# The last layer's weights padded to the full array, and the state's turn spread over VectorE and GpSimd, in a two-stage feed-forward of a four-stage layer kernel

## What is computed

```python
def ffn(x, ...):                      # x: [8, 1024, 256], normalized
    gf = global_net(x.mean(axis=1, keepdims=True), ...)       # one number per batch
    out = x
    for _ in range(3):
        h = gelu(out @ w1 + b1)       # 256 -> 256
        h = gelu(h @ w2 + b2)         # 256 -> 128
        h = gelu(h @ w3 + b3)         # 128 -> 64
        tf = sigmoid(h @ w4 + b4)     # 64 -> 1: one number per token
        c = 0.1 + adaptive_range * (0.7 * gf + 0.3 * tf - 0.5) * 2.0
        o_r, o_i, p_r, p_i = split(out, 4)
        out = out + c * concat([p_r, -p_i, -o_r, o_i])
    return out
```

## Time and profile before

| | |
|---|---|
| time of three runs | 3188.64, 3192.45, 3194.84 us; median 3192.45 |
| profiled execution | 3188.64 us; span from first to last instruction 3186.8 us |
| granted TensorE clock, mean of the span | 0.961 |
| busy in the span | TensorE 2836.8 us (89%), ScalarE 2018.3 (63%), VectorE 1842.2 (58%), GpSimd 1304.6 (41%) |
| the two ffn stages | about 950 to 1336 us and 2798 to 3187 us of the span |

### The profile page before, as it was taken

The page is one execution under the profiler, slowest core; times in us unless marked ns, Lnnn a source line. Parts: engine busy times, 40 slices in busy tenths (PEclk is TensorE's granted clock), DMA queues, the critical chain, the costliest instruction groups (busy, mean ns, idle before and its releaser), DMA issues. The chain is left out here.

```text
span 3186.8 us, 38521 instructions
## 1 busy us (share of the span) xinstructions
PE 2836.8 (89%) x12161; PEld 1226.6 (38%) x12161; DVE 1842.2 (58%) x2419; ACT 2018.3 (63%) x2642; POOL 1304.6 (41%) x795
## 2 busy tenths in 40 slices
PE   1799999999988999655999999999999999969998
PEld 0355555555553444331323232323333332234443
DVE  7899999999974453454354444444534442044444
ACT  4554555455434555424979797888878888935554
POOL 7699898889872220051313132222213230021210
PEclk8899999999998999867999999999999999989999
DMA  2000011001003220205463553545462717231112
GB/s 79 0 30 27 23 39 33 26 20 39 20 24 110 67 66 29 88 14 109 51 133 54 103 85 78 92 85 93 72 115 47 126 27 146 27 113 42 64 53 66
DMA packets 164017, 200.46 MB, mean 63 GB/s; under 512 B 16504, under 2 KB 118272, under 8 KB 163840
## 3 DMA queue, kind: packets, MB, share of 16 engines
q1 hardware_dynamic: 163840, 198.25, 28.2%
HBM read 139.49 MB, written 58.72 MB: 62 GB/s over the span
## 5 line engine op out<-in xcount | busy, mean ns | idle before, releaser
L1819 ACT ACTIVATE b_pr<-b_ps 128x1024 f32<-128x1024 f32 x1024 | 1003.0, 1025 | 256.0 <-PE b_ps L1916 251.6
L1916 PE MATMUL b_ps<-b_st 128*128 128x512 bf16 x2048 | 591.8, 386 | 71.1 <-DMA b_st<-b_scratch 33.9
L1898 PE MATMUL b_acc<-b_pr,b_vaug 128*32 128x512 f32 x4096 | 548.6, 608 | 0.4 <-ACT b_pr L1819 0.4
L1916 PEld LDWEIGHTS b_ps<-b_st 128*128 128x128 bf16 x2048 | 150.5, 98 | 649.2 <-ACT b_pr L1819 380.3
L1217 PE MATMUL f_po<-f_s,f_w 128*128 128x512 f32 x768 | 352.0, 600 | 10.1 <-DVE f_xr L1002 6.3
L990 DVE TENSOR_TENSOR f_turned<-f_cs,f_s 128x1024 f32<-128x1024 f32 x96 | 119.4, 1244 | 364.7 <-ACT f_cs L1119 359.7
L604 PE MATMUL a_pv<-a_xnT,a_wv 128*128 128x512 f32 x512 | 249.9, 612 | 48.2 <-DVE a_mem L389 31.4
L596 PE MATMUL a_pu<-a_xnT,a_wk 128*128 128x512 f32 x512 | 237.4, 607 | 36.2 <-DVE a_frac L350 30.3
L1083 ACT ACTIVATE f_h<-f_po,f_b 128x512 f32<-128x512 f32 x192 | 131.9, 687 | 215.8 <-PE f_po L1217 215.8
L1535 POOL TENSOR_TENSOR b_SQ<-b_A 128x1024 f32<-128x1024 f32 x32 | 64.7, 2022 | 466.9 <-DVE b_A L1632 466.9
L643 PE MATMUL a_py<-a_wo,a_out 128*128 128x256 f32 x960 | 228.3, 381 | 0.0
(11 more groups left out here) (247 smaller groups left out, 4659.2 us busy)
## 6 DMA issues: line engine op xcount, KB each, us to landing
b_st<-b_scratch SPq DMA_DIRECT2D x512, 128.0 KB, 6.9
b_scratch<-b_parts SPq DMA_DIRECT2D x32, 768.0 KB, 8.2
f_xl<-x SPq DMA_DIRECT2D x16, 1024.0 KB, 5.5
f_xr<-x SPq DMA_DIRECT2D x16, 1024.0 KB, 6.8
a_xl<-in_L_attn_a_x_dram SPq DMA_DIRECT2D x16, 512.0 KB, 4.3
x<-a_xr SPq DMA_DIRECT2D x32, 256.0 KB, 2.2
x<-f_xr SPq DMA_DIRECT2D x8, 1024.0 KB, 4.5
b_xl<-x SPq DMA_DIRECT2D x8, 1024.0 KB, 7.7
```

What stands on the lines that cost most here:

```text
L1819: nc.scalar.activation(pr[:, 4 * (blk % 2) + j, :], ps[:, j % 2, :], ACT.Exp, scale=SC).then_inc(S["probs_done"], 1)
L1898: x = nc.tensor.matmul(acc[32 * j:32 * j + 32, h * 512:(h + 1) * 512], vaug[:, kt, c:c + 32], pr[:, 4 * (kt % 2) + j, h * 512:(h + 1) * 51 ...
L1916: x = nc.tensor.matmul(ps[:, j % 2, h * 512:(h + 1) * 512], st[:, g % 2, 1, j, kt * P:(kt + 1) * P], st[:, g % 2, 0, j, h * 512:(h + 1) * ...
```

## The change

- w4r becomes two tiles of 128 rows, each with w4 on one half of the partitions and zeros on the other; GpSimd clears it first. L4's matmuls then use all 128 rows of the array and of h3.
- The coupling moves from ScalarE (L1119) to VectorE, as a tensor_scalar ahead of the turn.
- The turn no longer makes both products in one instruction. VectorE makes the product for row 0 right into the next state and adds to it; GpSimd makes the product for row 1 into the next state, and VectorE subtracts it from the state. GpSimd waits for the coupling, VectorE's subtract waits for GpSimd (b_done).
- GpSimd's turns stand in its queue in the order of the steps, between the normalizations; the last pair, in which GpSimd had nothing to do, has turns now too.
- `turned` and `couple` are gone.

```diff
-        w4r = s.sb("w4r", [P, P])
+        w4r = s.sb("w4r", [P, 2, P])
...
-        turned = s.sb("turned", [P, 2, KD, HT])
...
+                nc.gpsimd.memset(w4r[:], 0.0).then_inc(setup_p, 1)
...
+                def turn(x, k, j):                                          # GpSimd
+                    for h in range(NH):
+                        c = slice(h * HT, (h + 1) * HT)
+                        pool.wait_ge(cs_done[x], 6 * j + 2 * k + h + 1)
+                        nc.gpsimd.tensor_tensor(S[k + 1][:, x, 1, c], cs[:, x, c], S[k][:, x, 0, c],
+                                                ALU.mult).then_inc(b_done[x], 1)
+
                 def pair(j, first=False, last=False):
                     for step, x, k in ffn_steps(first, last):
+                        if step in ("L34", "L4"):
+                            turn(x, k, j - 1 if (x, k) == (1, 2) else j)
                         if step == "LN":
                             norm(x, j + 1)
...
+                pair(PAIRS - 1, last=True)
+                turn(1, 2, PAIRS - 1)
...
-                def turn(x, k, j):
+                def turn(x, k, j, end=False):                               # VectorE
...
-                        dve.wait_ge(cs_done[x], n + 1)
+                        dve.wait_ge(act_done, PRO + ACT_TILES * (j + (1 if (x, k) == (1, 2) else 0)) + (h + 2 if end else l34_at(x, k, 1 + h) + 1))
+                        dve.wait_ge(k2_done, j + 1)
...
-                        nc.vector.tensor_tensor(turned[:, h], cs[:, x, c].unsqueeze(1).broadcast_to([P, KD, HT]), src[:, x, :, c],
-                                                ALU.mult).then_inc(product_done[x], 1)
-                        dve.wait_ge(product_done[x], n + 1)
-                        nc.vector.tensor_tensor(dst[:, x, 0, c], src[:, x, 0, c], turned[:, h, 1, :], ALU.add)
-                        nc.vector.tensor_tensor(dst[:, x, 1, c], src[:, x, 1, c], turned[:, h, 0, :], ALU.subtract).then_inc(state_done[x], 1)
+                        nc.vector.tensor_scalar(cs[:, x, c], th[:, x, c], k1, k2[:, x:x + 1], ALU.mult, ALU.add).then_inc(cs_done[x], 1)
+                        dve.wait_ge(cs_done[x], n + 1)
+                        nc.vector.tensor_tensor(dst[:, x, 0, c], cs[:, x, c], src[:, x, 1, c], ALU.mult).then_inc(a_done[x], 1)
+                        dve.wait_ge(a_done[x], n + 1)
+                        nc.vector.tensor_tensor(dst[:, x, 0, c], dst[:, x, 0, c], src[:, x, 0, c], ALU.add)
+                        dve.wait_ge(b_done[x], n + 1)
+                        nc.vector.tensor_tensor(dst[:, x, 1, c], src[:, x, 1, c], dst[:, x, 1, c], ALU.subtract).then_inc(state_done[x], 1)
...
-                nc.vector.tensor_scalar(w4r[:], ones[:], w4c[:], None, ALU.mult).then_inc(setup_v, 1)
+                for h in range(2):
+                    r = slice(h * M3, (h + 1) * M3)
+                    nc.vector.tensor_scalar(w4r[r, h, :], ones[r, :], w4c[r, :], None, ALU.mult).then_inc(setup_v, 1)
...
-                    nc.scalar.activation(th[:, x, c], p, ACT.Tanh, scale=0.5, bias=hb4).then_inc(act_done, 1)
-                    act.wait_ge(k2_done, j + 1)
...
-                    nc.scalar.activation(cs[:, x, c], th[:, x, c], ACT.Identity, scale=k1, bias=k2[:, x:x + 1]).then_inc(cs_done[x], 1)
...
                 def l4(x, h, bank):
-                    r = slice(h * M3, (h + 1) * M3)
-                    nc.tensor.matmul(po[:, bank, :], w4r[r, :], h3[r, x, :], start=True, stop=True).then_inc(tile_ready, 1)
+                    nc.tensor.matmul(po[:, bank, :], w4r[:, h, :], h3[:, x, :], start=True, stop=True).then_inc(tile_ready, 1)
```

More of the change, by code:

```diff
@@ L825, in phase_f @@
         cs_done = [s.sem(f"cs_done{x}") for x in range(2)]
-        product_done = [s.sem(f"product_done{x}") for x in range(2)]
+        a_done = [s.sem(f"a_done{x}") for x in range(2)]
+        b_done = [s.sem(f"b_done{x}") for x in range(2)]
         state_done = [s.sem(f"state_done{x}") for x in range(2)]
@@ L1036, in _ @@
                 dve.wait_ge(w_loaded, N_W)
-                dve.wait_ge(setup_p, 4)
+                dve.wait_ge(setup_p, 5)
                 dve.wait_ge(setup_v, 2)
@@ L1044, in _ @@
                 nc.vector.tensor_scalar(hgb3, hgb3, 0.5, None, ALU.mult).then_inc(setup_v, 1)
-                nc.vector.tensor_scalar(w4r[:], ones[:], w4c[:], None, ALU.mult).then_inc(setup_v, 1)
+                for h in range(2):
+                    r = slice(h * M3, (h + 1) * M3)
+                    nc.vector.tensor_scalar(w4r[r, h, :], ones[r, :], w4c[r, :], None, ALU.mult).then_inc(setup_v, 1)
                 nc.vector.tensor_scalar(gw3r[0:M3, :], ones[0:M3, :], gw3c[0:M3, :], None, ALU.mult).then_inc(setup_v, 1)
-                dve.wait_ge(setup_v, 9)
+                dve.wait_ge(setup_v, 10)
                 pair(0, first=True)
@@ L1051, in _ @@
                 pair(PAIRS - 1, last=True)
-                turn(1, 2, PAIRS - 1)
+                turn(1, 2, PAIRS - 1, end=True)
                 for x in range(2):
@@ L1094, in pair @@
                                 p = take(j, at + h + (step == "L34"))
-                                couple(x, h, 6 * jj + 2 * k + h, jj, p, PRO + ACT_TILES * j + l34_at(x, k, 1 + h) + 1)
+                                n = 6 * jj + 2 * k + h
+                                if not isinstance(n, int) or n >= 2:
+                                    act.wait_ge(cs_done[x], n - 1)
+                                nc.scalar.activation(th[:, x, h * HT:(h + 1) * HT], p, ACT.Tanh, scale=0.5, bias=hb4).then_inc(act_done, 1)
                         if step == "inT":
@@ L1107, in pair @@
                         at += tiles_of(step, kind)
[L1109 to L1113, removed]
-                    nc.scalar.activation(th[:, x, c], p, ACT.Tanh, scale=0.5, bias=hb4).then_inc(act_done, 1)
-                    act.wait_ge(k2_done, j + 1)
-                    if not isinstance(n, int) or n >= 2:
-                        act.wait_ge(product_done[x], n - 1)
-                    act.wait_ge(act_done, tanh_at)
-                    nc.scalar.activation(cs[:, x, c], th[:, x, c], ACT.Identity, scale=k1, bias=k2[:, x:x + 1]).then_inc(cs_done[x], 1)
                 def g_step(j, i):
@@ L1132, in _ @@
                 act.wait_ge(w_loaded, N_W)
-                act.wait_ge(setup_v, 9)
+                act.wait_ge(setup_v, 10)
                 g_step(0, 0)
@@ L1144, in _ @@
                     p = take(PAIRS, 1 + h)
-                    couple(1, h, 6 * PAIRS - 2 + h, PAIRS - 1, p, PRO + ACT_TILES * PAIRS + 2 + h)
+                    act.wait_ge(cs_done[1], 6 * PAIRS - 3 + h)
+                    nc.scalar.activation(th[:, 1, h * HT:(h + 1) * HT], p, ACT.Tanh, scale=0.5, bias=hb4).then_inc(act_done, 1)
             @block.tensor
@@ L1270, in _ @@
                 pe.wait_ge(w_loaded, N_W)
-                pe.wait_ge(setup_v, 9)
+                pe.wait_ge(setup_v, 10)
                 g_step(0, 0)
```

## The result

The changed kernel takes 3246.95 us (median of 4 runs, 3242.39 to 3249.0); the kernel before, beside it, 3193.64. The ratio is 1.0165, 95% interval 1.015 to 1.018: 53 us slower. The profiled execution has a span of 3244.6 us.

A forecast was written before the change was run, and what follows sets the result against it. TensorE's queue was taken to bound the kernel. First pair 2.3, two middle pairs 16, last pair -0.8 and end 0 gave 17.5 us a stage, 35 for two stages, so 3226 us as measured; range 3199 to 3244.

The forecast's parts named there:

- L4 on the full array: Feed-forward stages: padded L4 takes 1.72 us instead of 1.25, +0.47 a step, about 11 us a stage, 22 in all.
- I take the 0.4 of L1645, so 3.05 a half: Turn on VectorE and GpSimd: disturbance between them adds 0.4 us to 2.65, so each half of a batch takes 3.05.
- the rival of full turns: Turn: VectorE and GpSimd fully alternate, 3.62 us a half, 50 us in all, 3242 us; chance 0.18, including worse.
- The last pair: Last pair of a feed-forward stage, without normalization on GpSimd: the change in time was put at -0.8 us.
- the end of a stage: Last turn of a feed-forward stage: done at +7.9 us behind L4 both before and after, so 0.
- each middle pair: The two middle pairs of a feed-forward stage: each was to grow by 8.0 us, 16 together.
- the gain of 0.5: Four L4 steps a stage without transposes or global net behind them: waits for the state go, each -0.5 us.
- GpSimd's queue: Middle pairs: GpSimd's product queues behind the normalization, making the two steps 3.2 and 3.1 us longer; thought to decide.
- No wait for a state behind the other turns: Sign: TensorE waits for a state only behind turns (0,0) and (1,0) of the middle pairs, some 2 to 3 us.
- The clock: Sign against the forecast: TensorE's granted clock falling below 1.00 in the inner stretches over the new waits.
- The rival that only TensorE pays: GpSimd's queue is not late, only the padded L4 costs: 3.4 us a stage, 7 in all, 3199 us; chance 0.16.
- The faster one: Padded L4 costs no more and the shorter chain frees waits: 7 us a stage, 14 in all, 3178 us; chance 0.04.

The follow-up runs named there:

- the padding alone: The kernel before with only L4 padded to the full array, coupling and turn as they were: 3203.05 us, ratio 1.0037.
- the array's halves back: The changed kernel with L4 on 64-row halves of the array again: 3241.83 us, ratio 1.0158.
- the experiment with the wait first: The changed kernel, but VectorE waits for GpSimd's product before its own product instead of before the subtract: 3273.22 us, one run.
- the experiment without GpSimd's product: The changed kernel with both products of the turn on VectorE and only the normalizations on GpSimd: 3208.57 us, ratio 1.0052.
- the experiment with the product first: The changed kernel with each normalization on GpSimd put behind the products of the next turn instead of ahead: 3217.06 us, ratio 1.0082.

## Why the prediction was wrong

The sign, the place and the order of causes were right; the sum was 35 us and the result 53, outside the range by 3. By its steps, L4 to L4 in the first stage:

- *L4 on the full array.* Right in its size: 1.72 us. The prediction has 11 a stage for it with nothing to cover it; under the waits that stand there the padding alone is worth 6.8 by the profiles and 12 us in the runs, against the 7 and 14 that were worked out for that experiment, with the result known. L4(0,2), with the global net's second step behind it, is 0.75 dearer, not 0.47 (13.63 to 14.38, with the padding alone too).
- *The term that failed* is "I take the 0.4 of L1645, so 3.05 a half". It is 3.69 in every undisturbed turn, more even than the 3.62 that I gave the rival of full turns. Two sizes in it were off. GpSimd's product is 1.27 us alone, not the half of a 1.89: the 1.89 is of an instruction with one tensor as both inputs, and the one with two, L1538 in the same trace, takes 2.37 in the median, whose half is 1.19. And the two engines don't share but take turns. The last pair went from -0.8 to +2.8, the first from 2.3 to 4.3, each middle pair from 8.0 to 9.2 (in it the step with the last turn of a pair, from +0.3 to +1.1), and the end of a stage from 0 to +1.1, since the last state is late as well. That is 9 us a stage, 18 in all, the size of the miss; 2.4 of the 9 have two other causes, named with the gain of 0.5 below, and 6.6 are left for the halves.
- *GpSimd's queue.* Right, in mechanism and size. Without the clock's fall, in the second stage, the two steps of the first middle pair grew by 3.7 and 2.8 (19.65 and 17.26 against 15.97 and 14.47); 3.2 and 3.1 were worked out. The normalization takes 5.32 us, since VectorE falls silent, and TensorE waits 1.9 for the state and 1.4 to 2.3 for the bank. That L1a starts at +8.93, where +8.95 was worked out for the state, is luck in part: the normalization was done at +6.9, 0.3 sooner than the +7.2, and the product was 0.3 longer than the 0.97. The queue's worth, taken off last, is 12.8 a stage, half of the change.
- *The gain of 0.5 in four steps* became a loss of 0.7 in the first and of 0.1 in three, only in part from the same term. The prediction took all of the 1.0 us by which these steps are over 12.7 for waits for the state. The rows show 0.37 of that; another 0.3 to 0.4 in three of the four, behind L4(0,0) of the first pair and L4(1,0) and L4(0,1) of the last, is TensorE waiting for its own L4 in the skipped step, which no shorter turn ends. With both products on VectorE these three are 13.76, 13.76 and 13.77, with no wait for a state and no gain: 0.5 each, 1.6 a stage, was never there. The fourth, behind L4(1,1), has no such wait, and there it is 13.22, the forecast gain. L4(0,2)'s 0.28 in three steps is the other 0.8 of the 2.4. "No wait for a state behind the other turns" held in three of the four, though in the first of them TensorE waits 0.42 for VectorE's queue instead; 0.16 came behind L4(1,1) of the last pair, and 1.0 behind L4(1,0) of the first, which has the normalization in it.
- *The clock.* I said that a fall below 1.00 would make it wrong. It did fall, in three of the four middle pairs, and cost nothing in this kernel: where it fell, the two steps are 21.37 and 15.46 us, 36.83 together; in the one pair where it stayed, these are 19.65 and 17.26:

```profile
2974.92 1.98 PE L1227 MATMUL f_po<-f_s,f_w 128*128 128x512 f32 x4 [1.85 <-DVE f_s L1011]
2979.20 3.70 PE L1227 MATMUL f_po<-f_s,f_w 128*128 128x512 f32 x8 [2.30 <-DVE f_xr L1019]
2982.83 1.08 PE L1179 MATMUL f_po<-f_h,f_w 128*64 128x512 f32 x4
2983.84 1.98 PE L1227 MATMUL f_po<-f_s,f_w 128*128 128x512 f32 x4
2985.66 1.88 PE L1184 MATMUL f_po<-f_h,f_w4r 128*128 128x512 f32 x4
...
2994.51 5.65 PE L1227 MATMUL f_po<-f_s,f_w 128*128 128x512 f32 x12 [1.79 <-DVE f_s L1011]
```

36.91. The engine at full clock reached the next wait sooner and waited longer: 1.79 for the second batch's state at 2994.51, where the slowed ones don't wait at all, and 2.30 for the bank, where the one slowed ahead of it waits 1.37. The chain over GpSimd and VectorE sets this stretch, and not TensorE. A fall behind the last of the waits does cost, as the 1.4 us with the array's halves back show.

The rivals: the one of full turns was nearly the truth, 3242 for 3247, and I gave it 0.18. That its 3.62 a half is so near the 3.69 is luck: with the measured 1.27, full turns would be the prediction's 2.65 for VectorE and 1.27, that is 3.92, and the engines overlap for 0.23 of it. The rule of the Trainium skill that stood beside it ("SBUF — State Buffer", Who interferes with whom: a VectorE instruction with two SBUF inputs and a GpSimd instruction that reads SBUF, each holding the other off) agrees with what the experiment with the wait first measured, but for that overlap. I preferred a mean over L1645, in which GpSimd was mostly not at work, to the one row that showed the case itself, GpSimd's normalization at 1.5 us beside the turn. L1645's own instructions, in the trace of the kernel before, are of two kinds:

```profile
L1645 DVE TENSOR_TENSOR b_SQ<-b_EP,b_SQ x32: 1224/1226/2726, 1375.5 to 2574.9; 128x1024 f32<-128x1024 f32 x32
...
1508.00 2.27 POOL L1535 TENSOR_TENSOR b_SQ<-b_A 128x1024 f32<-128x1024 f32 x1 [9.57 <-DVE b_A L1632]
...
1508.95 2.40 DVE L1645 TENSOR_TENSOR b_SQ<-b_EP,b_SQ 128x1024 f32<-128x1024 f32 x1 [0.43 <-ACT b_SQ L1794]
```

21 of the 32 take 1.23 us, and no instruction of GpSimd runs beside them; 11 take 2.24 to 2.73, and each of them started beside one, as the one shown did, which ends 1.08 behind it. The mean of 1.64, 0.4 over 1.24, describes none of them: the price of meeting GpSimd was 1.0 to 1.5 us, and that could be read before the change was made. The rival that only TensorE pays comes nearest to the experiment without GpSimd's product, at 3209, ten over its 3199. The faster one fell with the padding alone, 12 us slower.

The two profiled spans differ by 57.8 us. Of it 50.8 lie between the first and last L4 of the stages and 2.2 at their ends. The rest is 2.1 us ahead of the first L4, most of it from attention a, which no line of the change touches, and 2.9 at the start of the second stage, where the first L1's 16 records took 10.08 us in place of 7.13, with the granted clock at 0.50 over 2853 to 2857. The way from the last L4 of one stage to the first of the next is 1522.5 us before, 1526.4 after, and between 1521.7 and 1526.1 in the eight experiments, so this is no part of the change.

## What to carry over

When a vector operation on tensors in SBUF is split between VectorE and GpSimd, price it as if the two took turns; the split here cost 5 us a stage even with the normalizations out of its way. A mean over instructions hides this: look at minimum, median and maximum before taking a price from a row. Before giving an in-order engine a short job on the critical path, look what long job of it falls in the same microseconds, and order it behind. And when an engine waits a microsecond or two for its own input, as VectorE for the tanh, a later job whose input is ready fits in: that was worth 0.25%.

## What the runs showed of the hardware

GpSimd's product and VectorE's operations on 128x512 float32 in SBUF take 1.27, 0.69 and 0.69 us apart and 1.77, 0.69 and 1.64 side by side, in all turns alike of the experiment with the product first. Beside GpSimd's normalization VectorE's product and add take 0.93 each, and its coupling, which reads one such tensor, 0.55 to 0.85 where it is 0.55 elsewhere. In attention b of the kernel before, a VectorE instruction of 1024 columns with both inputs in SBUF (L1645) takes 1.23 with GpSimd silent and 2.24 to 2.73 where it meets a GpSimd instruction of 2.27. Two L4 matmuls on 64-row halves of the array take 1.06 us side by side, against 1.72 on the full array, but their first half is ready 0.1 us later. And the granted clock fell to 0.67 over 4 us right behind a TensorE wait of 1.9 us in a stream that was otherwise dense, and was back at 1.00 some 8 us later; in two other middle pairs it fell (0.85 and 0.79) behind the later wait for the bank, and with waits of 1.85 and 2.30 us in the second stage's first middle pair it did not fall. These rows don't show what decides it.
